# The opening of an attention kernel: batch 0 projected in plain fp32, with one token tile's queries ahead of it

## The chip, the cores and the metric

The program runs on one core of a Trainium2 chip. The metric is the device time of one launch, in microseconds (us): the median of three runs before the change is 610.33 us (609.41 to 612.26). Names of engines: PE is the tensor engine's matmul side and PEld its weight load, DVE is the vector engine, ACT the scalar engine, POOL the GpSimd engine, SP the sync engine, which here only issues loads and stores. ACT issues some loads as well.

## The reference

The program is one transformer-like block on `x` of 64 x 32 x 256 (64 batches of 32 tokens) and a context of 64 x 257 x 192, in three stages, each on a layer norm of `x` and added to it:

```
q = layernorm(x) @ Wq + bq           # 16 heads of 16
k = ctx @ Wk + bk ; v = ctx @ Wv + bv
attn = softmax(clip(q k^T / 4)) ; x = x + (attn v) @ Wo + bo
x = x + causal_attention_with_tanh(layernorm(x))     # second stage
x = x + mixture_of_8_experts(layernorm(x), top 2)    # third stage
```

Only the start of the first stage is touched here.

## The kernel before

The first stage goes over 64 batches `i`, one after the other. For one batch PE computes the scores (`scores(i)`, 16 instructions), weighs the values of batch `i-2` (`weigh`), transposes the probabilities of batch `i-1` (`transp`), and projects keys and values of batch `i+1` (`kproj`, `vproj`). DVE clips the scores, takes the negative maxima and copies half of the transposed probabilities; ACT computes the exponentials and moves keys, values and the other half out of PSUM; POOL spreads the queries over the heads' rows (`spread`, tile QF), handles the 257th key (`tailpart`, tile tm) and prepares the context.

In the loop keys and values are not multiplied as plain fp32. Context `cx` and weights `wA` are each cut into a high part (hA, wH) and a rest (lA, wL) of a faster format (fp32r), and five products stand for one (`terms`): 10 instructions for the keys and 10 for the values of a batch. The high parts are copies; the rests need a subtraction after them. `split(j, n)` on POOL does so for context pair `j` (two batches) in four steps n = 0 to 3: two high parts, the rest of channels 0 to 127, the rest of the last 64. A plain fp32 product is two instructions per pair of operands.

Ahead of the loop the kernel before does this. SP and ACT issue the loads in a written order; each has a queue of its own, and all share the core's 16 DMA engines. PE runs six products of 512 columns on a tile of ones (`warm(6)`). When the first four token tiles of `x` (512 tokens, batches 0 to 15) are there, DVE and POOL normalise them (`stats`, `rstd`, `xnorm`), PE turns them (`qturn(0)`), ACT copies them to `xnT` (`qchunk(0)`), PE computes the "x" row block, which is the 257th value of all batches, and then projects the queries of the 512 tokens (`qproj(0)`). DVE moves them to `qT` (`qevac(0)`). Only then do the projections of batch 0 follow, in the split form, and the loop starts. `base_row` is a small product of the output weights, done in iteration 0. The 257th values go to DRAM and come back spread over partitions (`load_tails`, tile Vt); POOL's `tailpart(0)` needs them.

Every engine runs its instructions in written order, and semaphores join the engines: `s_q`, `s_qe` for queries made and moved, `s_t0`, `s_t0e` for turned tokens, `s_wl` for the weights' rest, `s_lo` for the context's, `s_xn` for normalised token tiles. PSUM banks 4 to 7 go round in the order of the list `uses`; `take` on PE waits until the use four places earlier has been moved out.

## Time and profile before

| quantity | value |
|---|---|
| median of the runs | 610.33 us |
| time of the profiled execution | 609.9 us |
| its span, first to last instruction | 608.1 us |
| PE busy | 588.9 us (97% of the span) |
| DVE / ACT / POOL busy | 457.2 / 337.2 / 321.3 us |
| mean granted clock of PE | 0.994 |

The span and the time differ by 1.8 us, which lies around the instructions. In the page's 40 slices PE stands at 9 in each of the first 27, and the granted clock at 9 as well. So busy shares do not tell what bounds the opening; the chain of waits and the instructions in order of time do.

### The profile page before, as it was taken

The numbers are of one execution on the slowest core, as the hardware profiler recorded it, in microseconds if no ns is written. First come the engines' busy times: TensorE is split into PE (matmuls) and PEld (weight loads), VectorE is DVE, ScalarE is ACT, GpSimd is POOL, SyncE is SP. The second block draws the span as 40 slices with busy tenths as digits, with TensorE's granted clock in tenths as the row PEclk, the third lists the DMA queues.
The fourth block names the chain that finished last, engine by engine and source line by source line (L and its number), as shares of the span: only waits on it lengthen the run. The fifth ranks groups of instructions, "written<-read, shape, count | busy, mean of one in ns | idle before, by whom it ended". The sixth has DMA issues, their size and how long they took to land.

```text
span 608.1 us, 21788 instructions
## 1 busy us (share of the span) xinstructions
PE 588.9 (97%) x8367; PEld 482.3 (79%) x8367; DVE 457.2 (75%) x1069; ACT 337.2 (55%) x751; POOL 321.3 (53%) x474
## 2 busy tenths in 40 slices
PE   9999999999999999999999999998899999998977
PEld 4888878888788887888887788884588888884865
DVE  4688877888678886777777676888788888883654
ACT  3677868878687786777776156454323333330211
POOL 3457858787578777678874311111433333314771
PEclk9999999999999999999999999998999999999899
DMA  8724653776354855875400797257333334434884
GB/s 226 182 74 110 172 180 99 246 183 212 110 193 127 246 157 175 199 230 153 150 16 3 307 416 285 67 178 253 128 131 130 131 130 133 131 124 131 232 251 118
DMA packets 66069, 102.11 MB, mean 168 GB/s; under 512 B 15504, under 2 KB 42192, under 8 KB 65072
## 3 DMA queue, kind: packets, MB, share of 16 engines
q1 hardware_dynamic: 60672, 86.42, 44.2%
q0 software_dynamic: 4432, 13.50, 8.1%
q8 instruction: 69, 1.13, 0.8%
q10 hardware_dynamic: 864, 0.79, 0.5%
q14 instruction: 32, 0.26, 0.1%
HBM read 69.42 MB, written 31.26 MB: 166 GB/s over the span
## 4 chain that ended last, share of the span: by engine, by line
PE 54%; POOL 23%; issue 14%; DVE 3%; DMA 2%; ACT 2%; POOLq 0%; DVEq 0%; ACTq 0%
PE bank L1936 12%; PE scores L1936 6%; PE bank L1044 5%; PE bank L1051 5%; PE bank L1076 4%; POOL hA L718 4%; POOL lA L714 4%; POOL cg L1768 4%; POOL hA L710 4%; PE scores L1092 3%; PE scores L1065 3%; POOL Mb L751 2%; POOL tm L742 2%; PE bank L1961 1%; PE scores L1921 1%
## 5 line engine op out<-in xcount | busy, mean ns | idle before, releaser
L850 DVE TENSOR_SCALAR Pm<-scores 128x514 f32<-128x514 f32 x128 | 88.0, 688 | 52.8 <-PE scores L1065 52.6
L966 ACT ACTIVATE Pm<-Pm,nm 128x257 f32<-128x257 f32 x256 | 115.8, 505 | 2.5 <-DVE nm L855 2.5
L855 DVE TENSOR_REDUCE nm<-Pm 128x2 f32<-128x514 f32 x128 | 87.4, 683 | 2.2
L1757 POOL DMA_INDIRECT Xg<-y_d,inv x39 | 37.0, 950 | 82.9 <-PE scores L1921 70.1
L961 ACT ACTIVATE PT<-bank 128x512 f32<-128x512 f32 x64 | 38.3, 598 | 74.0 <-PE bank L1076 74.0
L1044 PE MATMUL bank<-hA,wH 128*128 128x258 f32 x256 | 75.2, 304 | 0.3 <-POOL hA L718 0.3
L1076 PE MATMUL bank<-cst,Pm 128*128 128x128 f32 x512 | 70.0, 279 | 0.0
L1044 PE MATMUL bank<-hA,wL 128*128 128x258 f32 x256 | 69.3, 281 | 0.0
L1051 PE MATMUL bank<-wH,hA 128*128 128x256 f32 x256 | 69.0, 281 | 0.0
L1051 PE MATMUL bank<-wL,hA 128*128 128x256 f32 x256 | 68.9, 280 | 0.0
L1895 ACT ACTIVATE sg<-sg 128x512 f32<-128x512 f32 x39 | 24.7, 632 | 77.6 <-DVE sg L1782 77.6
L1936 PE MATMUL bank<-W,xh 128*128 x208 | 66.7, 402 | 0.5 <-DVE xl L1849 0.5
L1092 PEld LDWEIGHTS scores<-Vs,PT 128*32 128x32 f32 x4096 | 41.2, 110 | 25.2 <-issue 24.1
L751 POOL TENSOR_TENSOR Mb<-Os,rc 128x64 f32<-128x64 f32 x64 | 21.6, 338 | 73.6 <-DVE rc L875 73.2
L1076 PEld LDWEIGHTS bank<-cst,Pm 128*128 128x128 f32 x512 | 54.9, 141 | 2.9 <-issue 0.8
L944 ACT ACTIVATE kT<-bank,bcol 128x258 f32<-128x258 f32 x128 | 53.5, 469 | 2.6 <-PE bank L1044 2.3
L1044 PEld LDWEIGHTS bank<-hA,wH 128*128 128x128 f32 x256 | 48.4, 189 | 1.2 <-issue 1.1
L1044 PEld LDWEIGHTS bank<-hA,wL 128*128 128x128 f32 x256 | 48.5, 189 | 0.2 <-issue 0.2
L1051 PEld LDWEIGHTS bank<-wL,hA 128*128 128x128 f32 x256 | 48.2, 188 | 0.0
L1051 PEld LDWEIGHTS bank<-wH,hA 128*128 128x128 f32 x256 | 48.2, 188 | 0.0
L1092 PE MATMUL scores<-Vs,PT 128*32 128x17 f32 x4096 | 47.5, 186 | 0.2 <-issue 0.2
L1768 POOL DMA_INDIRECT cg<-g_d,pi x32 | 31.7, 992 | 26.5 <-DMA g_d<-gg 17.0
(280 smaller groups left out, 1434.1 us busy)
## 6 DMA issues: line engine op xcount, KB each, us to landing
w_d<-whl SPq DMA_DIRECT2D x64, 256.0 KB, 3.5
W<-w_d SPq DMA_DIRECT2D x6, 2048.0 KB, 16.7
g_d<-gg SPq DMA_DIRECT2D x39, 256.0 KB, 2.4
wst<-in_W1T SPq DMA_DIRECT2D x32, 256.0 KB, 3.3
cx<-in_ctxT SPq DMA_DIRECT2D x31, 258.0 KB, 3.0
cx<-in_ctxT SPq DMA_DIRECT2D x62, 129.0 KB, 3.5
bb<-in_b SPq DMA_DIRECT2D x8, 512.0 KB, 6.3
W<-w_d SPq DMA_DIRECT2D x5, 512.0 KB, 5.3
```

The lines of the kernel that those rows point to most:

```text
L850: v.tensor_scalar(Pm[:, i % 2, 2 * p:2 * p + 2, :], S4[:, 2 * p:2 * p + 2, 0:NK], -CLAMP, CLAMP, ALU.max, ALU.min).then_inc(s_cl, 1)
L855: v.tensor_reduce(nm[:, i % 2, 2 * p:2 * p + 2], Pm[:, i % 2, 2 * p:2 * p + 2, :], AX.X, ALU.max, negate=True).then_inc(s_nm, 1)
L944: a.activation(kT[:, i % 2, m, :], held("k", i, m)[:, 0:NKP], ACT.Identity, bias=bcol[:, 2 + m:3 + m]).then_inc(s_ke, 1)
L961: a.activation(PT[:, i % 2, 0, :, :].rearrange("p a b -> p (a b)"), held("p", i, 0)[:, :], ACT.Copy).then_inc(s_pte[0], 1)
L966: a.activation(Pm[:, i % 2, g, :], Pm[:, i % 2, g, :], ACT.Exp, bias=nm[:, i % 2, g:g + 1]).then_inc(s_ex, 1)
L1044: mm = t.matmul(b[:, 0:NKP], w[:, 128 * m:128 * m + 128], c, start=(e == 0), stop=(e == 4))
L1051: mm = t.matmul(b[:, C * c:C * c + C], x[:, 128 * c:128 * c + 128], w[:, C:2 * C], start=(e == 0), stop=(e == 4))
L1076: mm = t.transpose(b[:, o:o + 128], Pm[:, i % 2, 2 * p + gg, 128 * c:128 * c + 128], ident)
L1092: mm = t.matmul(pO[r, VH * g:VH * g + VH], PT[:, i % 2, p, 2 * gg + c, r], Vs[:, i % 4, c, 4 * (h // 2) + g, h % 2, :], start=first, stop= ...
L1757: g.indirect_dma_start(out=Xg[:, i % 3, :], out_offset=None, in_=y_d, in_offset=bass.IndirectOffsetOnAxis(ap=inv[:, i:i + 1], axis=0)).the ...
L1768: g.indirect_dma_start(out=cg[:, j % 8, k, :], out_offset=None, in_=g_d, in_offset=bass.IndirectOffsetOnAxis(ap=pi[:, k, j:j + 1], axis=0) ...
L1936: mm = t.matmul(o, x[:, i % 2, k, :], W1[:, bass.DynSlice(w + (part * 2048 + k * 1024 + 512 * h), 512)], start=(k == 0 and part == 0 and x ...
```

## The change

Batch 0 no longer goes through the split form. Its context (columns of batch 0 alone), the key and value weights in plain fp32 and the biases are loaded first, with one token tile of `x` (tokens 0 to 127, batches 0 to 3) right behind; PE projects keys and values of batch 0 from them (`first_projections`, two products of 128 and 64 rows each), then turns and projects that one token tile (`first_queries`), and scores(0) follow. `warm(6)` is `warm(2)`, and the `warm(1)` further on is gone. The "x" row block comes after scores(0), the other three token tiles are normalised, turned and projected between batches 0 to 2: their statistics in the middle of batch 0's DVE work, their turn at the end of PE's iteration 0 and their projection at the end of iteration 1. On POOL the high parts of context pair 0 are made as well (ACT did them), and the statistics of the three tiles go ahead of pair 1's rests. Some semaphores are merged and counts shifted, which moves nothing.

```diff
-                load_x(0)
-                sp.dma_start(cst[:, 0:C_MN], d["cst"][:, 0:C_MN]).then_inc(s_id, 16)
-                sp.dma_start(wA[:, 0, C:2 * C], d["Wv"][0:128, :]).then_inc(s_w, 16)
-                sp.dma_start(wA[0:64, 1, C:2 * C], d["Wv"][128:192, :]).then_inc(s_w, 16)
+                src = d["ctxT"]
+                sp.dma_start(cx[:, 0, 0, 0, :], src[0, 0:128, :]).then_inc(s_f, 16)
+                sp.dma_start(xa[:, 0, :], d["x"][0:4].rearrange("a b c -> (a b) c")).then_inc(s_fx, 16)
+                sp.dma_start(wA[0:64, 1, 0:C], d["Wk"][128:192, :]).then_inc(s_f, 16)
+                sp.dma_start(cst[:, 0:C_MN], d["cst"][:, 0:C_MN]).then_inc(s_c, 16)
+                sp.dma_start(bcol[:, :], d["bcol"]).then_inc(s_f, 16)
+                sp.dma_start(Wq[:, :, :], d["Wq"].rearrange("(k p) n -> p k n", p=128)).then_inc(s_c, 16)
+                sp.dma_start(wA[64:128, 1, 0:C], d["Wk"][128:192, :]).then_inc(s_w, 16)
+                sp.dma_start(wA[64:128, 1, C:2 * C], d["Wv"][128:192, :]).then_inc(s_w, 16)
                 sp.dma_start(c256[:, 0, :], d["c256"][0:128, :]).then_inc(s_w, 16)
                 sp.dma_start(c256[0:64, 1, :], d["c256"][128:192, :]).then_inc(s_w, 16)
-                sp.dma_start(Wq[:, :, :], d["Wq"].rearrange("(k p) n -> p k n", p=128)).then_inc(s_c, 16)
-                sp.dma_start(bcol[:, :], d["bcol"]).then_inc(s_c, 16)
-                sp.dma_start(wA[64:128, 1, C:2 * C], d["Wv"][128:192, :]).then_inc(s_w, 16)
+                sp.dma_start(xa[:, 1:4, :], d["x"][4:16].rearrange("(n a) b c -> (a b) n c", a=4)).then_inc(s_x[0], 16)
                 sp.wait_ge(s_cx[0], 48)
...
-                split(0, 2)
-                split(0, 3)
-                split(1, 2)
+                for n in range(3):
+                    split(0, n)
                 spread(0)
                 g.wait_ge(s_qb, 1)
+                split(0, 3)
+                spread(1)
+                g.wait_ge(s_qb, 2)
+                rstd(0)
+                split(1, 2)
                 split(1, 3)
                 for i in range(T + 2):
-                    if i + 1 < T:
+                    if 1 <= i < T - 1:
                         spread(i + 1)
...
                 v.memset(PT[:, 0, 0, :, :], 1.0).then_inc(s_fill, 1)
-                v.wait_ge(s_x[0], 16)
-                stats(0, 4)
-                v.wait_ge(s_mv, 4)
+                v.wait_ge(s_fx, 16)
+                stats(0, 1)
+                v.wait_ge(s_mv, 1)
                 v.wait_ge(s_rs, 1)
-                for n in range(4):
-                    xnorm(n)
-
+                xnorm(0)
+                first_qevac()
...
+                def first_tokens():
+
+                    v.wait_ge(s_vx, 1)
+                    v.wait_ge(s_v1, 1)
+                    for h in range(2):
+                        v.tensor_copy(vx[:, h, :, :, 0:16],
+                                      held("x")[0:T, 128 * h:128 * h + 128].rearrange("p (g s c) -> p s g c", g=4, s=2)
+                                      ).then_inc(s_vxe, 1)
+                    v.wait_ge(s_rs, 2)
+                    for n in range(1, 4):
+                        xnorm(n)
...
+                        if i == 0:
+                            v.wait_ge(s_x[0], 16)
+                            stats(1, 3)
...
                     if i == 0:
+                        first_tokens()
                         base_row()
+                    if i == 1:
+                        qevac(0)
...
+                def first_qchunk():
+                    a.wait_ge(s_t0, 1)
+                    a.activation(xnT[:, :, 0:128], held("first turn")[:, 0:256].rearrange("p (k n) -> p k n", k=2), ACT.Copy
...
-                src = d["ctxT"][0:2]
-                a.dma_start(cx[:, 0, 0, :, :], src[:, 0:128, :].rearrange("b p n -> p b n")).then_inc(s_cx[0], 16)
-                for h in range(2):
-                    a.dma_start(cx[64 * h:64 * h + 64, 0, 1, :, :], src[:, 128:192, :].rearrange("b p n -> p b n")
-                                ).then_inc(s_cx[0], 16)
...
-                highs(0)
-                qchunk(0)
-                a.wait_ge(s_w, 16 * 8)
-                a.activation(wH[:, :, :], wA[:, :, :], ACT.Copy).then_inc(s_wh, 1)
-                highs(1)
+                src = d["ctxT"]
+                a.dma_start(wA[:, 0, 0:C], d["Wk"][0:128, :]).then_inc(s_f, 16)
+                a.dma_start(cx[0:64, 0, 1, 0, :], src[0, 128:192, :]).then_inc(s_f, 16)
+                a.dma_start(wA[:, 0, C:2 * C], d["Wv"][0:128, :]).then_inc(s_fv, 16)
+                a.dma_start(wA[0:64, 1, C:2 * C], d["Wv"][128:192, :]).then_inc(s_fv, 16)
+                a.dma_start(cx[:, 0, 0, 1, :], src[1, 0:128, :]).then_inc(s_cx[0], 16)
+                a.dma_start(cx[0:64, 0, 1, 1, :], src[1, 128:192, :]).then_inc(s_cx[0], 16)
+                a.dma_start(cx[64:128, 0, 1, :, :], src[0:2, 128:192, :].rearrange("b p n -> p b n")).then_inc(s_cx[0], 16)
...
+                kevac(0, 0)
+                kevac(0, 1)
+                first_qchunk()
+                a.wait_ge(s_f, 80)
+                a.wait_ge(s_fv, 32)
+                a.wait_ge(s_w, 64)
+                a.activation(wH[:, :, :], wA[:, :, :], ACT.Copy).then_inc(s_wh, 1)
+                vevac(0)
+                highs(1)
...
-                warm(6)
+                warm(2)
...
+                def first_projections():
+
+                    t.wait_ge(s_f, 80)
+                    for m in range(2):
+                        b = take("k", 0, m)
+                        for k in range(2):
+                            K = 128 - 64 * k
+                            mm = t.matmul(b[:, 0:NKP], wA[0:K, k, 128 * m:128 * m + 128], cx[0:K, 0, k, 0, :],
+                                          start=(k == 0), stop=(k == 1))
+                        mm.then_inc(s_k, 1)
+                    t.wait_ge(s_fv, 32)
+                    b = take("v", 0)
+                    for c in range(2):
+                        for k in range(2):
+                            K = 128 - 64 * k
+                            mm = t.matmul(b[:, C * c:C * c + C], cx[0:K, 0, k, 0, 128 * c:128 * c + 128], wA[0:K, k, C:2 * C],
+                                          start=(k == 0), stop=(k == 1))
+                    mm.then_inc(s_v, 1)
+
+                def first_queries():
+
+                    t.wait_ge(s_c, 32)
+                    t.wait_ge(s_xn, 1)
+                    b = take("first turn")
+                    for k in range(2):
+                        mm = t.transpose(b[:, 128 * k:128 * k + 128], xa[:, 0, 128 * k:128 * k + 128], ident)
+                    mm.then_inc(s_t0, 1)
+                    t.wait_ge(s_t0e, 1)
+                    b = take("first q")
+                    for m in range(2):
+                        for k in range(2):
+                            mm = t.matmul(b[:, 128 * m:128 * m + 128], Wq[:, k, 128 * m:128 * m + 128], xnT[:, k, 0:128],
+                                          start=(k == 0), stop=(k == 1))
+                    mm.then_inc(s_q, 1)
+
...
+                def x_row():
+
+                    t.wait_ge(s_w, 64)
+                    b = take("x")
+                    for k in range(2):
+                        K = 128 - 64 * k
+                        mm = t.matmul(b[0:T, 0:C], c256[0:K, k, :], wA[0:K, k, C:2 * C], start=(k == 0), stop=(k == 1))
+                    mm.then_inc(s_vx, 1)
+
+                first_projections()
+                first_queries()
...
-                t.wait_ge(s_wl, 1)
-                for i in range(-1, T + 2):
-                    if 0 <= i < T:
+                for i in range(T + 2):
+                    if i < T:
                         scores(i)
+                    if i == 0:
+                        x_row()
+                        t.wait_ge(s_wl, 1)
...
+                    if i in turns:
+                        qturn(turns.index(i))
+                    if i - 1 in turns:
+                        qproj(turns.index(i - 1))
```

PE, from the warm-up to the first scores, or the first split product where these come later. `bank` is a PSUM bank, cst the unit matrix, c_79 the 257th context rows, hA and lA, wH and wL the parts. Before:

```order
L1003 MATMUL bank<-PT 128x512 x5
L1020 MATMUL bank<-cst,xb 128x128 [waits s_xn,s_id]
L1020 MATMUL bank<-cst,xb 128x128 [waits s_xn] x7
L1003 MATMUL bank<-PT 128x512
L1112 MATMUL bank<-wA,c_79 64x256 [waits s_w,s_c]
L1112 MATMUL bank<-wA,c_79 64x256
L1029 MATMUL bank<-xnT,Wq 128x512 [waits s_t0e]
L1029 MATMUL bank<-xnT,Wq 128x512
L1029 MATMUL bank<-xnT,Wq 128x512 [waits s_t0e]
L1029 MATMUL bank<-xnT,Wq 128x512
L1044 MATMUL bank<-hA,wH 128x258 [waits s_lo,s_t0e,s_wl]
```

Now:

```order
L1054 MATMUL bank<-PT 128x512
L1164 MATMUL bank<-cx,wA 128x258 [waits s_f]
L1164 MATMUL bank<-cx,wA 128x258 x3
L1172 MATMUL bank<-wA,cx 128x256 [waits s_fv]
L1172 MATMUL bank<-wA,cx 128x256 x3
L1182 MATMUL bank<-cst,xb 128x128 [waits s_xn,s_c]
L1182 MATMUL bank<-cst,xb 128x128
L1188 MATMUL bank<-xnT,Wq 128x128 [waits s_ke,s_t0e]
L1188 MATMUL bank<-xnT,Wq 128x128 x3
L1118 MATMUL scores<-kT,QF 64x258 [waits s_ke,s_qb]
L1118 MATMUL scores<-kT,QF 64x258 x7
L1198 MATMUL bank<-wA,c_79 64x256 [waits s_ke,s_w]
```

What stood before the first split product was the work of four token tiles and the "x" block; now plain projections and one token tile stand there, and the scores of batch 0 precede the "x" block. The turn of the three other tiles and their projection have gone behind `base_row` and behind the projections of batch 2.

DVE, around the work of batch 0. Pm and nm are its clipped scores and maxima, st and mv statistics, xb the tokens. Before:

```order
L816 TENSOR_SCALAR qT<-bank,bcol 128x512 [waits s_q] x2
L850 TENSOR_SCALAR Pm<-scores 128x514 [waits s_s]
L855 TENSOR_REDUCE nm<-Pm 128x2 [waits s_cl]
L850 TENSOR_SCALAR Pm<-scores 128x514 [waits s_s]
L855 TENSOR_REDUCE nm<-Pm 128x2 [waits s_cl]
L841 TENSOR_TENSOR base<-bank,bcc 128x256 [waits s_base,s_c2]
L850 TENSOR_SCALAR Pm<-scores 128x514 [waits s_s]
```

Now:

```order
L890 TENSOR_REDUCE nm<-Pm 128x2 [waits s_cl]
L885 TENSOR_SCALAR Pm<-scores 128x514 [waits s_s]
L825 BN_STATS st<-xb 128x6 [waits s_x0]
L825 BN_STATS st<-xb 128x6 x2
L828 BN_AGGR mv<-st 128x2 [waits s_st] x3
L890 TENSOR_REDUCE nm<-Pm 128x2 [waits s_cl]
L865 COPY vx<-bank 64x8x16 [waits s_v1,s_vx]
L865 COPY vx<-bank 64x8x16
L831 SCALAR_TENSOR_TENSOR xb<-xb,mv,rs 128x256 [waits s_rs]
L831 SCALAR_TENSOR_TENSOR xb<-xb,mv,rs 128x256 x2
L876 TENSOR_TENSOR base<-bank,bcc 128x256 [waits s_base,s_w3]
L885 TENSOR_SCALAR Pm<-scores 128x514 [waits s_s]
```

Statistics of three tiles stand between the clip and the second maximum of batch 0, and the "x" copies and three normalisations between that maximum and batch 1.

POOL, from the end of the first normalisation to the loop. Before:

```order
L714 TENSOR_TENSOR lA<-cx,hA 128x516 [waits s_hi,s_cx0,s_rs]
L718 TENSOR_TENSOR hA<-cx,hA 64x516 [waits s_lo]
L714 TENSOR_TENSOR lA<-cx,hA 128x516 [waits s_hi,s_cx1,s_lo]
L728 TENSOR_TENSOR QF<-qT,cst 128x128 [waits s_qe]
L718 TENSOR_TENSOR hA<-cx,hA 64x516 [waits s_lo,s_qb]
L728 TENSOR_TENSOR QF<-qT,cst 128x128 [waits s_lo]
L728 TENSOR_TENSOR QF<-qT,cst 128x128 [waits s_s]
```

Now:

```order
L724 TENSOR_SCALAR hA<-cx 128x516 [waits s_f,s_cx0]
L724 TENSOR_SCALAR hA<-cx 128x516
L731 TENSOR_TENSOR lA<-cx,hA 128x516 [waits s_fhi,s_cx0]
L747 TENSOR_TENSOR QF<-qT,cst 128x128 [waits s_qe]
L735 TENSOR_TENSOR hA<-cx,hA 64x516 [waits s_lo,s_qb]
L747 TENSOR_TENSOR QF<-qT,cst 128x128 [waits s_lo]
L689 TENSOR_TENSOR rs<-mv,epw 128x3 [waits s_mv,s_qb]
L691 TENSOR_TENSOR rs<-rs,epw 128x3 [waits s_ep]
L731 TENSOR_TENSOR lA<-cx,hA 128x516 [waits s_hi,s_cx1,s_rs]
L735 TENSOR_TENSOR hA<-cx,hA 64x516 [waits s_lo]
```

The three tiles' rstd (lines 689, 691) waits for DVE's statistics, and the rests of pair 1 are queued behind it.

## Rows read from the trace of the kernel before

**Rows 1.** The chain that ended last, 0 to 60 us: start, us, what.

```profile
9.70 0.77 PE bank L1020 x5
...
12.47 3.63 PE bank L1029 x8
16.11 1.20 PE bank L1044 x10
17.30 1.18 PE bank L1051 x10
18.48 0.62 PE scores L1065 x16
...
21.67 0.86 PE bank L1122 x4
22.53 0.62 PE scores L1065 x16
23.15 1.02 PE bank L1076 x8
...
26.56 0.62 PE scores L1065 x16
```

**Rows 2.** Waits of PE, 16 to 326 us: us in total, times, longest.

```profile
PE scores L1065 <- POOL QF L728: 0.6, 2, 0.3
```

**Rows 3.** Weight loads of the warm-up in order of time: start, us.

```profile
1.44 0.50 PEld L1003 LDWEIGHTS bank<-PT 128*128 128x128 f32 x2 [1.44 <-DVE PT L819]
...
5.87 0.34 PEld L1003 LDWEIGHTS bank<-PT 128*128 128x128 f32 x1 [0.52 <-issue]
6.55 0.19 PEld L1003 LDWEIGHTS bank<-PT 128*128 128x128 f32 x1 [0.34 <-issue]
```

**Rows 4.** Loads of the opening: KB, us from issue to landing.

```profile
cst<-in_cst SPq DMA_DIRECT2D x1, 84.0 KB, 3.8
...
wA<-in_Wk ACTq DMA_DIRECT2D x1, 64.0 KB, 5.4
bcol<-in_bcol SPq DMA_DIRECT2D x1, 4.0 KB, 5.8
...
cx<-in_ctxT SPq DMA_DIRECT2D x1, 258.0 KB, 3.0
```

**Rows 5.** DMA issues on SP and ACT in order of time: start, us.

```profile
5.31 0.59 SPq L579 DMA_DIRECT2D wA<-in_Wv  x1
...
18.17 3.79 SPq L604 DMA_DIRECT2D Vt<-vx_d  x8
...
4.50 0.62 ACTq L933 DMA_DIRECT2D wA<-in_Wk  x1
```

**Rows 6.** DVE in order of time: start, us, line, tiles, idle time before.

```profile
4.76 1.40 DVE L802 BATCH_NORM_STATS2 st<-xb 128x6 f32<-128x256 f32 x4 [3.37 <-DMA xb<-in_x]
...
7.97 1.67 DVE L808 SCALAR_TENSOR_TENSOR xb<-xb,mv,rs 128x256 f32<-128x256 f32 x4 [1.53 <-POOL rs L688]
12.13 1.50 DVE L828 TENSOR_TENSOR wL<-wA,wH 128x1024 fp32r<-128x1024 f32 x1 [2.48 <-ACT wH L937]
13.55 0.47 DVE L832 COPY vx<-bank 64x128 f32<-64x128 f32 x2
...
19.15 0.69 DVE L850 TENSOR_SCALAR Pm<-scores 128x514 f32<-128x514 f32 x1 [2.25 <-PE scores L1065]
```

**Rows 7.** POOL and ACT in order of time, the same columns.

```profile
6.81 1.04 POOL L688 TENSOR_TENSOR rs<-rs,epw 128x4 f32<-128x4 f32 x1
9.91 1.29 POOL L714 TENSOR_TENSOR lA<-cx,hA 128x516 fp32r<-128x516 f32 x1 [2.05 <-ACT hA L922]
...
16.97 0.40 POOL L728 TENSOR_TENSOR QF<-qT,cst 128x128 f32<-128x128 f32 x1 [0.92 <-DVE qT L816]
...
23.38 1.23 POOL L710 TENSOR_SCALAR hA<-cx 128x516 fp32r<-128x516 f32 x2
...
10.06 1.09 ACT L917 ACTIVATE xnT<-bank 128x512 f32<-128x512 f32 x2 [0.33 <-PE bank L1020]
```

More of the change, by code:

```diff
@@ L224, in build @@
         pO = S4[:, 3, 272:272 + 4 * VH]
-        uses = [(("t", 0, k), s_t0e, k + 1) for k in range(2)] + [(("x",), s_vxe, 2)] + [(("q", 0, m), s_qe, m + 1) for m in range(2)]
-        for i in range(-1, T + 1):
+        turns = (0, 11, 27, 43)
+        uses = [(("k", 0, p), s_ke, p + 1) for p in range(2)] + [(("v", 0), s_ve, 1)]
+        uses += [(("first turn",), s_t0e, 1), (("first q",), s_qe, 2), (("x",), s_vxe, 2)]
+        for i in range(T + 1):
             if 1 <= i:
@@ L235, in build @@
                 uses += [(("b",), s_basee, 1)]
-            if 0 <= i < 48 and i % 16 == 11:
-                uses += [(("t", i // 16 + 1, k), s_t0e, 2 * (i // 16 + 1) + k + 1) for k in range(2)]
-            if 0 <= i < 48 and i % 16 == 12:
-                uses += [(("q", i // 16 + 1, m), s_qe, 2 * (i // 16 + 1) + m + 1) for m in range(2)]
+            if i in turns:
+                uses += [(("t", turns.index(i), k), s_t0e, 2 * turns.index(i) + k + 2) for k in range(2)]
+            if i - 1 in turns:
+                uses += [(("q", turns.index(i - 1), m), s_qe, 2 * turns.index(i - 1) + m + 3) for m in range(2)]
         spot = {u[0]: n for n, u in enumerate(uses)}
@@ L967, in exps @@
                                  ).then_inc(s_ex, 1)
-                for i in range(-1, T + 1):
+                kevac(0, 0)
[7 more added lines that the diff above has]
+                highs(1)
+                for i in range(T + 1):
                     if 1 <= i:
@@ L982, in _ @@
                         vevac(i + 1)
-                    if 0 <= i < 48 and i % 16 == 11:
-                        qchunk(i // 16 + 1)
+                    if i in turns:
+                        qchunk(turns.index(i))
                     q = (i - 8) // 3
@@ L1102, in busy @@
                                  skip_group_check=True)
-                t.wait_ge(s_id, 16)
-                qturn(0)
-                warm(1)
-                t.wait_ge(s_c, 32)
-                t.wait_ge(s_w, 16 * 8)
-                b = take("x")
-                for k in range(2):
-                    K = 128 - 64 * k
-                    mm = t.matmul(b[0:T, 0:C], c256[0:K, k, :], wA[0:K, k, C:2 * C], start=(k == 0), stop=(k == 1))
-                mm.then_inc(s_vx, 1)
-                qproj(0)
+                def first_projections():
[15 more added lines that the diff above has]
+                    mm.then_inc(s_v, 1)
@@ L1149, in _ @@
                         base_row()
-                    if 0 <= i < 48 and i % 16 == 11:
-                        qturn(i // 16 + 1)
-                    if 0 <= i < 48 and i % 16 == 12:
-                        qproj(i // 16 + 1)
+                    if i in turns:
+                        qturn(turns.index(i))
+                    if i - 1 in turns:
+                        qproj(turns.index(i - 1))
             @block.sync
```

101 lines of the change are left out of this document (56 added, 45 removed).

## The prediction

> **What bounds the kernel now.** I read three views. The chain of waits tells which engine's work ended last at each moment. From 9.70 us on it lies on PE without a break: the turn of four token tiles, the query projection of 512 tokens at 12.47 (eight instructions, 3.63 us), keys and values of batch 0 from 16.11 to 18.48, then scores(0) at 18.48, scores(1) at 22.53 and scores(2) at 26.56 [rows 1]. The waits say the same of the loop: from 16 to 326 us PE's longest entry is 0.6 us over two waits [rows 2]. So the loop of 64 batches is pure PE time, and a change of the opening is worth what it moves scores(2) by, the first scores behind which both programs have the same work left. Everything is settled in the first 28 us, and I read DVE, POOL, ACT and the loads there in order of time.
>
> The measure is therefore the start of scores(2): 26.56 us before.
>
> **When the first product can start now.** It waits for five loads, the biases last of SP's. Issues follow one another by about 0.55 us (SP's ninth ends at 5.9, having begun at 0.72) [rows 5], so the biases are issued near 2.9. A load issued in the opening crowd takes 3.8 us (84 KB) to 5.8 us (the biases themselves, behind 1.1 MB on their queue), and 3.0 us (258 KB) when the crowd has passed [rows 4]. With 0.41 MB ahead of it on its queue I take the quickest, 3.0: the start is at 5.9, bounds 5.9 and 8.7. It can't be before 4.9, where the warm-up ends: two products are four instructions of 512 columns, one per 0.85 us from 1.44 on [rows 3]. The value weights, issued fourth on ACT near 3.2, land at 6.2 to 8.6, inside or just behind the key projection.
>
> **What the first projections cost.** Plain fp32 has eight instructions for the keys and eight for the values, 256 or 258 columns. Four of 256 columns took 0.86 us (line 1122) [rows 1], 0.215 each, so 3.44 us at the high clock; the split form took 1.20 + 1.18 = 2.38. The plain form is 1.06 us dearer on PE, and is bought for an earlier start. The clock matters more. The warm-up's weight loads stand 0.85 us apart up to 5.87 and take 0.34 us, and take 0.19 from 6.55 [rows 3]: by that pace PE runs at its lower level (1.2 GHz) for some 4.8 us of unbroken work from 1.44 and at 2.4 GHz afterwards, though the granted clock reads 0.99 for the whole. In the old opening that slow stretch was filler and cost nothing. Now PE works to 4.9, stands idle for a microsecond and then does real work. If the rise comes at 6.6 all the same, the sixteen instructions end at 5.9 + 3.44 + 0.35 = 9.7. If it takes another 4.8 us from 5.9, eleven run at 0.43, and they end at 11.7. No row shows which; I take a rise at 8.0 (about five instructions at 0.43, eleven at 0.215), ending at 10.4, nearer the early end because the filler still counts for something.
>
> The Trainium skill's page "TensorE: Matmul & The Clock Gate", section "What's actually happening", says that "the default state is throttled, and activity releases the throttle." The trace agrees in that the pace doubles only after sustained work, and it speaks against cutting the warm-up from six to two. By that rule alone the late end, 11.7, would hold.
>
> **One token tile's queries.** Two turns at 0.128 (eight took 1.02) [rows 1]: 10.65. ACT copies 256 columns, two of 512 took 1.09 [rows 7], so 0.35: 11.05. Eight instructions of 128 columns, 0.128 each as for the turns: 12.1. DVE moves two blocks of 128 columns, as the two copies at 13.55, 0.5 us [rows 6]: 12.7. POOL's spread takes 0.40 [rows 7]: scores(0) starts at 13.2, hand-overs included. Beside this, POOL first makes two high parts (1.23) and one rest (1.29) [rows 7], from a load whose last piece is issued near 5.1 on ACT (the sixth of before was at 4.50 [rows 5]) and takes up to 5.4 us [rows 4]: done by 13.0 at the latest, so at worst 0.3 us late. The tile's normalisation (loads at about 5, then 0.35 + 0.1 + 0.3 + up to 1.04 + 0.42) ends by 7.3 and is covered by the projections. So scores(0) comes 5.3 us earlier than at 18.48.
>
> **What is owed afterwards.** The work that stood ahead of it comes between. After scores(0) at 13.2: scores 0.62, the "x" block 0.86 (four instructions of 256 columns like line 1122), keys and values of batch 1 2.38, `base_row` 0.86: PE is at 17.9. The rest of the weights must be there for batch 1's keys at 14.7: DVE has it at 12.7 + 1.50 = 14.2 [rows 6], POOL the context's at 13.2 + 1.28 = 14.5. Both just fit. wL also needs ACT's wH, whose last load is SP's tenth, issued near 5.9 and at most 5.8 us on its way: 11.7, plus half the price of ACT's two copies of 512 columns per 512, 1.1 for 1024, is 12.8, so in the worst case the keys come 0.1 late.
>
> Then PE must turn three token tiles, six times 0.128, and here it waits. DVE's chain: wL to 14.2, clip, maximum, clip (0.69 each, overlapping by 0.1) to 16.2, statistics of three tiles 1.05 (four took 1.40) and 0.3: 17.5. POOL's rstd, 0.2 and up to 1.04 (no row has three columns; four took 1.04, and I take that): 18.9. DVE fills the time with batch 0's second maximum and the "x" copies, then normalises three tiles at 0.42 (four took 1.67): 20.15 [rows 6, 7]. The second round of turns can only follow the third tile, so PE is through at 20.7 instead of 18.7. This is a new wait of 2.0 us, and behind it in PE's order stand scores(1).
>
> From 20.7: scores(1) 0.62, transposes 1.02, keys and values of batch 2 2.38, the projection of 384 tokens 2.6 (three quarters of 3.63 is 2.7; eight instructions at 0.32 are 2.6). scores(2) start at 27.3. POOL's rests of pair 1, queued behind the rstd, end at 18.9 + 2.6 = 21.5, ahead of 22.3 where they are wanted.
>
> Sum: 27.3 - 26.56 = +0.75 us. Check by amounts: the real work starts 3.8 us earlier (9.70 to 5.9). Against it stand 1.06 for the plain form and 0.2 for the small query products, 1.06 for the lower clock, 1.5 for the hand-overs between the first tile's turn and scores(0), and 2.0 for the three tiles' wait; 1.3 of filler and load waits, which the old stretch from 9.70 to 26.56 held beside 15.6 of work, falls away. That gives +0.7. The profiled execution (609.9, span 608.1 and 1.8 around it) becomes 610.65; the median of the runs is 0.43 above it, so I forecast 611.1.
>
> The other new order is hidden. The "x" copies end near 18.6 rather than 14.0. In the old trace the eight tail loads were issued by 21.96 (18.17 + 3.79) [rows 5], 7.9 behind the copies; now 26.5, and batch 2's first clip, which needs tile tm, is due at 28.0. That leaves about 1.2 us.
>
> **Rivals.**
> A. The loads land late and the clock is late: slower. Place: the first product's wait. If the biases take the 5.8 us of their own row, the start is 8.7, PE has been idle for 3.8 us, and eleven instructions run at the lower level: projections end at 14.5, 4.1 later than I take, everything behind shifts, and scores(2) start at 31.4, which is 615.2. For it: every load issued after 2.9 in the old opening took over 5 us, as the biases' and the key weights' rows show. Against: the queues carry much less ahead of these. It decides from a projection end of 12.7, where the loss passes 3.05 us.
>
> The Trainium skill's page "DMA: Bandwidth & Descriptors", section "Bandwidth", has the rule: "Transfers under 64 KB are descriptor-dominated." The rows agree that the 4 KB load was no quicker than one of 64 KB (5.8 against 5.4). This adds to A's chance and not to its price.
>
> B. The three tiles' wait does not arise and the clock rises early: faster. The projections end at 9.7 (-0.7), the loads at 4.9 (-1.0), and POOL and DVE are through with the tiles when PE arrives (-2.0 in full). All three together give 26.56 - 2.95, or 607.4; the early clock and half the wait give 609.4. For it: the chain of DVE is long but each piece is an estimate. Against: DVE's chain hangs on the same first scores as PE's, so an earlier start moves both and closes nothing.
>
> C. The 257th values come late: their round through DRAM takes 3 us more than 7.9. Then batch 2's clip waits 1.8 us, and PE behind it, 612.9.
>
> D. Nothing shows: losses and gains cancel within 0.3 us, 610.3. This belongs to the forecast's own range.
>
> **How the numbers follow.** The forecast with D has 0.65, A 0.13, B 0.15, C 0.07. A change of this kernel can be told from none at about 0.5%, or 3.05 us: below 607.3 or above 613.4. The forecast, its early clock (610.4) and late clock (612.4), C and nearly all of B lie inside. Faster is what B reaches at its full length, 0.06. Slower is A, nearly whole, with a sliver of C beside a late clock, 0.14. That leaves 0.80 within. The range goes from 608.2 (B in most parts) to 614.2 (A with half its delay).
>
> **What would show it.** In the new profile: the first fp32 product at 5.9, the pace of its instructions (0.43 or 0.215), scores(0) at 13.2, a wait of PE at line 1073 for DVE's normalised tiles of about 2 us, scores(1) at 20.7 and scores(2) at 27.3, and the same distances from there on. It is wrong if PE waits at batches 2 to 4, if that wait is missing, or if scores(2) differ from 27.3 by more than 2 us.

## The result and the profile after

The changed kernel takes 620.06 us, median of four runs (616.77 to 621.05), against 609.87 before (608.21 to 612.26; the 610.33 given ahead of the prediction was the median of the first three): ratio 1.0145, 95% interval 1.0112 to 1.0178. It is slower, and 5.9 us above the upper end of the forecast's range. The profiled execution took 620.06 with a span of 618.2. scores(2) start at 37.10 instead of 26.56 [rows 1], 10.5 us later. That is the whole difference of 10.2, and from there on the batches follow at the same distances as before. So the measure was the right one, and the size of every step ahead of it decides.

The chain that ended last (start, us, what) in the new kernel:

```profile
4.85 4.54 DMA cx<-in_ctxT
...
12.12 6.92 issue
...
19.07 1.32 POOL QF L747
...
20.43 1.18 PE scores L1118 x16
...
26.20 2.57 DVE xb L831 x2
...
29.84 0.66 PE bank L1073 x4
30.49 0.62 PE scores L1118 x16
...
37.10 0.62 PE scores L1118 x16
```

Before, the chain lay on PE from 9.70 on [rows 1]. Now it passes through POOL's spread (QF) and DVE's normalisation (xb), the hand-over ahead of scores(0) and the one that the change moved between scores(0) and scores(1). In the stretch from 12.12 the view stays with POOL, which has nothing to do there; QF's own row below names DVE's qT as what it waits for, and qT waits for PE's queries, which end at 18.34. So PE's work of the opening is on the path up to there. PE in order of time (start, busy us, line, tiles, idle time before):

```profile
5.88 4.69 PE L1164 MATMUL bank<-cx,wA 128*128 128x258 f32 x8 [0.65 <-DMA bcol<-in_bcol]
10.51 4.67 PE L1172 MATMUL bank<-wA,cx 128*128 128x256 f32 x8
15.11 0.69 PE L1182 MATMUL bank<-cst,xb 128*128 128x128 f32 x2
16.27 2.07 PE L1188 MATMUL bank<-xnT,Wq 128*128 128x128 f32 x8 [0.47 <-ACT xnT L963]
20.43 1.17 PE L1118 MATMUL scores<-kT,QF 32*64 32x258 f32 x16 [2.09 <-POOL QF L747]
21.53 2.16 PE L1198 MATMUL bank<-wA,c 128*64 128x256 f32 x4
...
23.99 0.42 PE L1097 MATMUL bank<-hA,wL 128*128 128x258 f32 x1
...
27.32 0.28 PE L1104 MATMUL bank<-wH,lA 128*128 128x256 f32 x1
...
27.68 1.02 PE L1209 MATMUL bank<-Wo,bcol 128*128 128x256 f32 x4
...
29.30 0.33 PE L1073 MATMUL bank<-cst,xb 128*128 128x128 f32 x1 [0.49 <-DVE xb L831]
29.84 0.66 PE L1073 MATMUL bank<-cst,xb 128*128 128x128 f32 x4 [0.21 <-DVE xb L831]
```

The sixteen plain instructions last from 5.88 to 15.11, 9.2 us. Scores(0) take 1.18 where they took 0.62 [rows 1], split products 0.42 each up to 27.1 and 0.28 behind it: PE runs at its lower level (1.2 GHz) for the first 21 us of its real work, while the granted clock of the profile reads 1.00 throughout. The first change of the clock that this trace records is the rise at 27.2, and ahead of it the view shows 1.00. A second profile of the same kernel, e11 below, records a change early on, and its granted clock is 0.50 where the same instructions take the same times. Stretch, its length, busy us of PE, PEld, DVE, ACT and POOL, granted clock, share and GB/s of DMA, in the kernel after, then in e11:

```profile
5.88:15.11 9.23, 9.23 (x17) 4.00 (x17) 0.00 (x0) 0.95 (x2) 2.49 (x3) 1.00 0.85 233
```

```profile
7.70:16.00 8.30, 7.83 (x16) 3.52 (x17) 0.00 (x0) 1.86 (x4) 2.50 (x3) 0.50 0.79 228
```

The weight loads of the first pairs show a second loss:

```profile
5.88 0.50 PEld L1164 LDWEIGHTS bank<-cx,wA 128*128 128x128 f32 x2 [2.23 <-DMA bcol<-in_bcol]
7.04 0.50 PEld L1164 LDWEIGHTS bank<-cx,wA 64*128 64x128 f32 x2 [0.66 <-issue]
8.19 0.50 PEld L1164 LDWEIGHTS bank<-cx,wA 128*128 128x128 f32 x2 [0.66 <-issue]
```

A plain product is a pair of instructions. One pair takes 1.155 us, and two instructions of 256 columns at the lower level take 0.86. The missing 0.30 is a weight load that isn't hidden: from pair to pair the operands change between 128 and 64 rows. DVE and POOL, the same columns:

```profile
18.91 1.22 DVE L858 TENSOR_TENSOR wL<-wA,wH 128x1024 fp32r<-128x1024 f32 x1
...
26.20 3.58 DVE L831 SCALAR_TENSOR_TENSOR xb<-xb,mv,rs 128x256 f32<-128x256 f32 x3 [0.38 <-POOL rs L691]
```

```profile
19.07 1.31 POOL L747 TENSOR_TENSOR QF<-qT,cst 128x128 f32<-128x128 f32 x1 [6.95 <-DVE qT L847]
...
25.27 0.89 POOL L691 TENSOR_TENSOR rs<-rs,epw 128x3 f32<-128x3 f32 x1
26.24 1.30 POOL L731 TENSOR_TENSOR lA<-cx,hA 128x516 fp32r<-128x516 f32 x1
27.61 1.34 POOL L735 TENSOR_TENSOR hA<-cx,hA 64x516 fp32r<-64x516 f32 x1
```

The spread took 0.40 before [rows 7]; now it begins 0.16 us behind wL and ends 0.25 behind wL's end. Four normalisations took 1.67 [rows 6]; three take 3.58, beside the rests of pair 1.

### The profile page after: what moved, and what is told of

Read it like the earlier page. It is cut to its first block, busy times and chain, and to the rows that moved or that the text cites. A ratio compares the mean times of both kernels' runs of the same rounds, so it can differ in the third digit from the quotient of the medians.

```text
span 618.2 us, 21790 instructions
## 1 busy us (share of the span) xinstructions
PE 595.5 (96%) x8361; PEld 483.3 (78%) x8361; DVE 459.2 (74%) x1071; ACT 336.4 (54%) x750; POOL 324.3 (52%) x478
## 4 chain that ended last, share of the span: by engine, by line
PE 48%; POOL 24%; issue 16%; DVE 8%; DMA 2%; ACT 2%; POOLq 0%; ACTq 0%; DVEq 0%
PE bank L2025 12%; PE scores L2025 6%; PE bank L1097 4%; PE bank L1104 4%; POOL cg L1857 4%; PE bank L1129 4%; POOL lA L731 4%; POOL hA L735 4%; POOL hA L724 4%; PE scores L1118 3%; PE scores L1145 3%; POOL Mb L770 2%; POOL tm L761 2%; PE scores L2010 1%; POOL whl L804 1%
## 5 line engine op out<-in xcount | busy, mean ns | idle before, releaser
L1118 PE MATMUL scores<-kT,QF 32*64 32x258 f32 x1024 | 44.7, 406 | 2.7 <-POOL QF L747 2.7
```

The lines of the kernel that those rows point to most:

```text
L1118: mm = t.matmul(B[g][64 * m:64 * m + 64, 0:NKP], QF[r, i % 2, m, :], kT[r, i % 2, m, :], start=True, stop=True, skip_group_check=True)
```

## The experiments

They ran on chips where the kernel before takes 629.2 to 629.4 us (the profiles of e3 and e7, which are that kernel with one change each, have the extra time in the last stage: behind line 1936 they have 76 us left, and the kernel before has 59 on the first chip; the distances between scores(0), (1) and (2) are as before), so each ratio is to the kernel before on the same chip. Starts of scores(0), (1), (2) are from each profile; "by start" is 629.3 plus what scores(2) start after 26.56, an estimate of the time from one profile. In the last two rows scores(2) lack a projection of 2.6 us that comes a batch later; it is added.

| run | median us | ratio (95%) | scores(0), (1), (2) | by start |
|---|---|---|---|---|
| e11_after_here | 636.36 | 1.0107 (1.0076–1.0138) | 19.7, 29.7, 36.3 | 639.1 |
| e1_warm6 | 636.84 | 1.0119 (1.0077–1.0160) | 18.2, 27.8, 34.4 | 637.1 |
| e2_warm4 | 634.57 | 1.0097 (1.0065–1.0129) | 15.6, 25.6, 32.3 | 635.0 |
| e3_before_warm2 | 631.38 | 1.0043 (1.0021–1.0066) | 20.2, 24.2, 28.2 | 631.0 |
| e4_grouped | 637.67 | 1.0120 (1.0066–1.0175) | 20.0, 30.1, 36.7 | 639.5 |
| e9_rows128 | 632.51 | 1.0065 (1.0044–1.0086) | 14.3, 23.9, 30.5 | 633.3 |
| e5_filled | 634.59 | 1.0086 (1.0062–1.0110) | 15.6, 25.9, 32.5 | 635.2 |
| e6_ports | 632.74 | 1.0063 (1.0040–1.0086) | 15.4, 24.2, 31.7 | 634.4 |
| e7_plain_only | 633.32 | 1.0069 (1.0047–1.0091) | 21.0, 25.0, 29.1 | 631.8 |
| e10_split_back | 638.85 | 1.0167 (1.0146–1.0187) | 20.3, 30.2, 36.8 | 639.5 |
| e8_all_mended | 631.51 | 1.0030 (1.0009–1.0051) | 14.9, 22.6, 27.3 + 2.6 | 632.7 |
| e12_reordered | 631.88 | 1.0041 (1.0020–1.0063) | 14.5, 19.3, 26.0 + 2.6 | 631.4 |

The last column agrees with the medians within 1.8 us for all but the unaltered kernel (2.7). That one's four runs were 634.0, 634.2, 638.5 and 639.3, and the profile is of the longest, which the estimate meets to 0.2; e4's four spread from 634.1 to 639.8 in the same way, and its profile is of the longest too. No profile of a quick execution of either was taken.

**The warm-up.** e1_warm6 and e2_warm4 alter one number, e3_before_warm2 makes the cut alone, in the kernel before:

```diff
-                warm(2)
+                warm(6)    (e1; warm(4) in e2)
-                warm(6)
+                warm(2)    (e3, kernel before)
```

> The changed kernel with the warm-up of before (six products instead of two). Theory (clock): the whole loss, 10.5 us at the start of scores(2), comes from PE staying at its lower level (1.2 GHz) from 5.9 to 27.1 us because the short warm-up never raised it. With six products the pace rises near 6.2 as in the kernel before, the plain products start near 8.7 and run at half the time (16 at 0.29 = 4.6 us, to 13.3), scores(2) start near 30 and the run takes about 613.5. Rival (products): the plain products with their gaps don't hold the level wherever they stand; the pace falls back to the lower level after the warm-up, scores(2) start near 37 and the run takes 620 or more.

> The changed kernel with four warm-up products. Theory (clock): the pace rises near 6.2, inside the seventh or eighth of eight instructions; the warm-up ends at 7.3, the plain products end near 11.9, scores(2) start near 28.8: about 612. Rival (products): as for six, 620. A second rival (size of the gap): what counts is whether PE ever stands idle before the rise; then this one behaves as with six, 1.5 us earlier.

> The kernel before with two warm-up products instead of six. Theory (clock): the first real work at 9.1 then runs at the lower level; turns, x block and the 512-column query products cost twice as much until the pace rises. If it rises 4.8 us into the 512-column products the loss is 2 to 4 us (612 to 614); if it stays low as in the changed kernel, 8 us (618). Rival (no clock): the warm-up is filler, and the time stays at 610.

Weight loads of e2:

```profile
4.78 0.19 PEld L1054 LDWEIGHTS bank<-PT 128*128 128x128 f32 x1 [0.27 <-issue]
...
6.06 0.19 PEld L1164 LDWEIGHTS bank<-cx,wA 128*128 128x128 f32 x1 [0.24 <-DMA bcol<-in_bcol]
...
7.02 0.29 PEld L1164 LDWEIGHTS bank<-cx,wA 64*128 64x128 f32 x2 [0.34 <-issue]
7.65 0.30 PEld L1164 LDWEIGHTS bank<-cx,wA 128*128 128x128 f32 x2 [0.34 <-issue]
```

All sixteen run at 2.4 GHz, from 6.49 to 11.42, 4.9 us instead of 9.2, and scores(0) come 4.1 us before e11's. In all six profiles with a warm-up of four or more and the plain form (e1, e2, e5, e6, e8, e12) they do so; of the four with two, only e9's. When the level rises differs from execution to execution: the first weight load of 0.19 us stands at 4.8 in e2, e5 and e7, at 5.7 in e12, at 6.4 in e6, at 6.5 in e1 and the kernel before, at 6.6 in e8 and at 7.5 in e10. Two products end at 5.2, ahead of most of these. So the cut of the warm-up is what leaves the projections' level to the execution. Behind them the level falls in both, in e2 during the 2.1 us wait for the spread, in e1 near 19.9, as the split products begin; scores(2) start at 32.3 and 34.4, not at the 28.8 and 30 expected, because the rest of the loss remains. With six products in e1 the filler also holds the first plain product back to 9.1; against e2 that costs 2.6 us at scores(0).

The medians do not show a gain: e11, unaltered, has 636.36, between e2's 634.57 and e1's 636.84, and the intervals overlap. Two of e11's four executions took 634, as e2's five did; that these two ran the plain products at the higher level is likely and was not profiled.

In e3 the same cut costs the kernel before 1.7 us at scores(2) and 2.2 at the median, clear of the noise (2 to 4 us were expected): there too the low stretch reaches real work (its pace rises near 13.4).

**The rows of the operands.** e4_grouped orders the same products by rows, so the row count changes three times instead of seven; e9_rows128 has 128 rows everywhere; it leaves the last 64 context channels out of batch 0 and counts the first 128 twice.

```diff
+                    bk = [take("k", 0, m) for m in range(2)]
+                    for k in range(2):
+                        for m in range(2):
...
-                        for k in range(2):
+                        for e, k in enumerate((1 - c, c)):
```

> The changed kernel with the plain products in another order: the products of 128 rows and those of 64 rows are grouped, so that the number of rows changes 3 times instead of 7. Theory (weight load): each change of the row count leaves a weight load of 0.3 us uncovered, which is why a pair of instructions takes 1.155 us instead of 0.853; with the grouping the sixteen take about 9.23 - 4 x 0.30 = 8.0 us, and everything behind comes 1.2 us earlier: 618.8. Rival (256 columns): at the lower level every pair of 256 columns pays 0.3, whatever the rows; the sixteen take 9.2 and the time stays at 620. If the denser stream raises the clock, 614 or less.

```diff
-                            mm = t.matmul(b[:, 0:NKP], wA[0:K, k, 128 * m:128 * m + 128], cx[0:K, 0, k, 0, :],
+                            mm = t.matmul(b[:, 0:NKP], wA[:, 0, 128 * m:128 * m + 128], cx[:, 0, 0, 0, :],
```

> The changed kernel (two warm-up products) in which the second half of each plain product reads the operands of the first half, 128 rows instead of 64; the last 64 context channels are thereby left out of batch 0's keys and values and the first 128 counted twice. Theory (row count): with no change of the row count no weight load stays uncovered: a pair of 256-column instructions takes 0.853 us at the lower pace, the sixteen 6.9 us instead of 9.2. Rival: the pair still takes 1.155. For the pace itself: if it rises within this stream of full products, about 5 us after it begins, the sixteen end near 12 and scores(2) start near 33; if it stays low as with the 64-row products, near 34.7.

e4's sixteen take 6.67 to 14.71, 8.04 us instead of 9.23: four changes fewer, 1.19 us, 0.30 each, as expected. Scores(0) still start no earlier than in e11, whose first four instructions ran at the higher level and whose sixteen take 8.03 as well, and the median is no better. At the higher level (e12) the same order takes 4.15 instead of 4.93, 0.20 each. e9's PE:

```profile
6.41 2.01 PE L1163 MATMUL bank<-cx,wA 128*128 128x258 f32 x8 [1.21 <-DMA bcol<-in_bcol]
8.25 1.89 PE L1170 MATMUL bank<-wA,cx 128*128 128x256 f32 x8
```

They end by the next turn at 9.98, 3.6 us from 6.41 on: an instruction takes 0.22, near the 0.215 of the prediction, for products of one row count at the higher level. e9 was also at that level from its first product, with warm(2). That isn't an effect of the rows alone, for the unaltered kernel, e11_after_here, began at it too:

> The changed kernel itself, unaltered, on the same chip as the other experiments, so that their ratios can be set beside its own. Every theory expects 1.014 to 1.017 of the kernel before and scores(2) near 37.

```profile
6.31 0.30 PEld L1164 LDWEIGHTS bank<-cx,wA 128*128 128x128 f32 x2 [2.65 <-DMA bcol<-in_bcol]
...
7.57 0.36 PEld L1164 LDWEIGHTS bank<-cx,wA 128*128 128x128 f32 x2 [0.34 <-issue]
8.59 0.50 PEld L1164 LDWEIGHTS bank<-cx,wA 64*128 64x128 f32 x2 [0.66 <-issue]
```

In that execution two pairs ran at 0.63, the third took 1.02 and the rest 1.155: the level fell inside the third, and the granted clock falls to 0.50 at 7.7, with PE working without a stop, where e2 and e9 kept theirs. In the kernel after, in e4 and in e11 it is then low to 27 or 28; in e9 it is low from 15.7 to 22.

**The plain form alone.** e7_plain_only gives the kernel before the plain products for batch 0, and nothing else of the change (one later load is moved to keep their operands).

```diff
+                    if i == 0:
+                        for k in range(2):
+                            K = 128 - 64 * k
+                            mm = t.matmul(b[:, 0:NKP], wA[0:K, k, 128 * m:128 * m + 128], cx[0:K, 0, k, 0, :],
```

> The kernel before, its warm-up, loads and four-tile queries as they were, with only batch 0's keys and values in plain fp32 (load_ctx(2) is issued after these products, since they read the plain context). Theory (weight load): at the high pace sixteen instructions with a change of the row count between pairs take 16 x 0.29 = 4.6 us to 5.0 against 2.38, so scores(2) start 2.3 to 2.6 us later: 1.0040. Rival (columns alone): 16 x 0.215 = 3.44, 1.1 us later.

```profile
12.45 3.70 PE L1030 MATMUL bank<-xnT,Wq 128*128 128x512 f32 x8
15.99 2.49 PE L1047 MATMUL bank<-cx,wA 128*128 128x258 f32 x8
18.41 2.58 PE L1061 MATMUL bank<-wA,cx 128*128 128x256 f32 x8
20.92 0.69 PE L1081 MATMUL scores<-kT,QF 32*64 32x258 f32 x16
```

At the higher level the sixteen take 4.93 us where the split form took 2.38 [rows 1], +2.5, and scores(0) to (2) are late by that. The prediction had +1.06. The median is 3.9 above the kernel before. PE stands still for another 1.3 us ahead of 31.9, with no engine named as what it waits for; whether that is the rest of the median is not shown, for the profiled execution itself is 2.6 above (632.04).

**Who decides scores(1).** e5_filled adds to e2 products that nobody reads (two behind the first queries, four ahead of the turn), so that the pace never falls.

```diff
+                        if c == 0 and k == 0:
+                            fill(b[:, :], 4)
...
+                    fill(B[0][:, :], 2)
```

> The kernel with four warm-up products (e2_warm4), and PE kept at work in its two long waits: two 512-column filler products behind the first queries' projection, four ahead of the turn of the three tiles (they write a bank that is overwritten afterwards). Theory (chain): the pace stays high from 6 us on, but behind the first queries the start of scores(1) hangs on DVE and POOL (scores(0), clip, wL, statistics, rstd, three normalisations), so only the first scores' shorter duration is won: scores(1) start 0.4 to 0.8 us earlier than e2's 25.6, scores(2) near 31.6, 4.6 to 5.2 us above the kernel before. Rival (clock): the lower pace between 15.6 and 22 us is most of e2's remaining loss of 5.7 us; then scores(2) start below 29 and the loss is under 2.5 us.

```profile
20.91 3.56 DVE L831 SCALAR_TENSOR_TENSOR xb<-xb,mv,rs 128x256 f32<-128x256 f32 x3 [0.38 <-POOL rs L691]
```

```profile
21.62 3.60 PE L1161 MATMUL bank<-PT 128*128 128x512 f32 x8
25.05 0.82 PE L1075 MATMUL bank<-cst,xb 128*128 128x128 f32 x6
```

From scores(0) to scores(1) it takes 10.2 us, in e2 with its pace falling 10.0. The filler itself costs some of that: the third normalisation ends at 24.47, and the turn starts behind the filler at 25.05. From the start of scores(0) to the end of the normalisations it is 8.8 us here and 9.3 in e2. So PE's pace is worth 0.5 us in this stretch, the difference between scores(0) of 0.71 and of 1.18, and the rest is DVE's and POOL's chain, which ends with three normalisations of 3.56.

e6_ports is e2 with DVE's wL held until the first spread is done, and POOL's rests of pair 1 until the normalisations are:

```diff
+                g.wait_ge(s_xn, 4)
...
+                v.wait_ge(s_qb, 1)
```

> e2_warm4 with DVE and POOL kept from working at the same time at two places: DVE's wL waits until POOL has spread batch 0's queries, and POOL's rests of pair 1 wait until DVE has normalised the three tiles. Theory (contention): the spread takes 0.40 instead of 1.31 us and the three normalisations 1.25 instead of 3.58; scores(0) start 0.9 earlier, scores(1) 3.0 earlier (22.6), PE then waits about 0.5 for the rests of pair 1, and scores(2) start near 29.7: 3 us above the kernel before. Rival (these operations are slow for another reason, the shape or PSUM): both keep their durations, the waits only add, and the loss is 6 to 7 us.

```profile
15.44 2.34 DVE L860 TENSOR_TENSOR wL<-wA,wH 128x1024 fp32r<-128x1024 f32 x1 [0.58 <-POOL QF L747]
...
22.24 1.28 DVE L832 SCALAR_TENSOR_TENSOR xb<-xb,mv,rs 128x256 f32<-128x256 f32 x3 [0.38 <-POOL rs L691]
```

```profile
14.93 0.40 POOL L747 TENSOR_TENSOR QF<-qT,cst 128x128 f32<-128x128 f32 x1 [1.69 <-DVE qT L848]
15.41 1.28 POOL L735 TENSOR_TENSOR hA<-cx,hA 64x516 fp32r<-64x516 f32 x1
```

The spread is back at 0.40 and the three normalisations at 1.28, so both had been waiting for the other engine. The same shows where it was moved to: wL, begun 0.03 us behind a rest of 1.28, takes 2.34 instead of 1.22. The Trainium skill's page "SBUF — State Buffer", section "SBUF: two separate sides", says that GpSimd and a DVE instruction with two inputs from SBUF share ports under an exclusive lock, and that the loser blocks until the other is through. The trace agrees: wL ends 1.1 us behind the end of the rest that was ahead of it, and in the kernel after QF ends 0.25 behind wL's end, neither more than the second one's own duration (1.22 and 0.40). Of the 3.2 us freed, 0.6 reach scores(2) against e2: the filler of this execution ran longer at the lower level, so the first product starts 0.7 later (7.21), and PE now waits 0.6 for wL, 1.6 for the "x" copies and 0.6 for a late rest. The expectation had scores(2) at 29.7; they start at 31.7.

**The queries' part alone.** e10_split_back keeps the single token tile and returns batch 0 to the split form, with warm(6).

```diff
-                  first_projections()
+                  t.wait_ge(s_wl, 1)
+                  for p in range(2):
+                      kproj(0, p)
+                  vproj(0)
```

> The changed kernel with its loads, one token tile first and the rest between batches, but batch 0 in the split form as before and six warm-up products: the plain part undone alone. Theory (the queries' part loses by itself): keys and values wait for wL and the context's rest near 15, scores(0) start near 17.4, the chain over DVE and POOL to the three tiles' turn takes its 9.5 us to scores(1) as with six warm-ups, scores(2) near 34: 7 us above the kernel before. Rival (the plain form is the culprit): scores(2) near 28, 1 to 2 us above the kernel before.

```profile
13.37 2.13 POOL L736 TENSOR_TENSOR hA<-cx,hA 64x516 fp32r<-64x516 f32 x1
```

```profile
PE bank L1097 <- POOL hA L736: 4.0, 1, 4.0
```

scores(0) start at 20.3, later than before and than the 17.4 expected: PE waits 4.0 us for the context's last rest on POOL, which itself takes 2.13 instead of 1.28 beside wL, and behind that wait the split products run at the lower level, 4.55 us instead of 2.38. Without the plain form the operands, made in series on POOL, are too late for an early start.

**Mended versions.** Both have warm(4) and grouped products, hold wL behind the first spread (e12 behind both), let POOL make the rests of pair 1 ahead of the three tiles' rstd, and turn the three tiles a batch later; e8 has one filler product behind the first queries; e12_reordered, without it, puts the "x" block into the wait for the spread, makes all parts of pair 0 ahead of it, and moves `base_row` and the statistics.

```diff
-        turns = (0, 11, 27, 43)
+        turns = (1, 11, 27, 43)
...
+                v.wait_ge(s_qb, 1)     (s_qb, 2 in e12)
```

> The changed kernel with every loss found so far taken out: four warm-up products, the plain products grouped by rows, wL behind the spread, one filler product in the wait for it, and the three tiles' rstd after the rests of pair 1 with their turn in iteration 1 and their projection in iteration 2 (so nothing on PE waits for them). Theory: scores(0) near 13.7, scores(2) near 23.7 with 2.6 us of query projection still owed behind them, that is 26.3 against 26.5 of the kernel before: the same time within 0.5 us. If another wait takes their place, 2 to 4 us slower.

> The changed kernel with what the experiments showed put right: four warm-up products; plain products grouped by rows; the x block in the wait for batch 0's spread queries; POOL makes all of pair 0's parts before that spread; wL waits for both spreads; base_row after batch 2's projections, so it needs no bank that DVE still holds; statistics of the three tiles at the end of DVE's batch 0, their normalisation in batch 1, turn at the end of PE's iteration 1, projection in iteration 2. Theory (sum of the parts measured): plain products from 6.5 to 10.5, scores(0) near 14, scores(2) near 24.3 with 2.6 us owed behind it, so 26.9 less what the x block saves: 0.5 to 2 us faster than the kernel before, ratio 0.997 to 0.999. Rival (some other wait of this opening takes its place, as with e8): 1.002 or more.

The waits of PE up to 40 us (us in total, times, longest) in e8, then in e12:

```profile
PE bank L1217 <- DVE vx L866: 1.5, 1, 1.5
PE bank L1055 <- DVE PT L850: 1.4, 1, 1.4
PE bank L1098 <- DVE wL L859: 0.6, 1, 0.6
```

```profile
PE bank L1104 <- DVE wL L860: 1.1, 1, 1.1
PE bank L1218 <- DVE PT L902: 0.9, 1, 0.9
```

They give back two thirds of the loss, and neither beats the kernel before (1.003 and 1.004, both intervals above 1); e12's theory, 0.997 to 0.999, missed. Read from the rows, and not parted by further runs, what stays is 1.8 us of dearer plain products (4.15 in e12 against 2.38), the uncovered pass from the first tile over ACT, PE, DVE and POOL to scores(0), and waits for DVE, which has the opening's work of before in a shorter stretch.

## Why the prediction was wrong

Profiled forecast and profile of after, in us from step to step:

| step | forecast | measured | off by |
|---|---|---|---|
| first plain product | 5.9 | 5.88 | 0.0 |
| plain products | 4.5 | 9.2 | +4.7 |
| their end to scores(0) | 2.8 | 5.3 | +2.5 |
| scores(0) to scores(1) | 7.5 | 10.1 | +2.6 |
| scores(1) to scores(2) | 6.6 | 6.6 | 0.0 |

- **"When the first product can start now" was right**, to 0.02 us. It took the quickest load of the old rows, and in this profile the biases landed after 3.0. Rival A's place, late loads, did not occur. Three profiles of the same head on the other chips start at 6.3, 6.4 and 6.7, so that meeting the bound to 0.02 was partly luck.
- **"What the first projections cost" failed, twice.** *The clock:* the step took a rise at 8.0, with 11.7 as its late bound, because PE had taken 4.8 us of unbroken work to rise [rows 3]. That was one execution's value; the others' rises lie between 4.8 and 7.5 on the clock of the trace. In the kernel after it rose at 27.1. Neither bound held the outcome, since both let the level rise within the step and stay. e11's fall at 7.7 under load shows that this is no safe assumption. The Trainium skill's page "TensorE: Matmul & The Clock Gate", section "What's actually happening", has activity release the throttle. By that rule the prediction put the end at 11.7; in this trace PE was busy for 9.2 us from 5.88 to 15.11 without a stop and stayed low, so the measurement decides against it. *The weight loads:* 0.215 an instruction came from line 1122, whose four instructions all have 128 rows. A row of the same chain, passed over, has two pairs of 128 and 64 rows:

```profile
11.33 1.15 PE bank L1112 x4
```

  0.575 a pair at the higher level instead of 0.43; by it the sixteen take 4.6, and e7 measured 4.93. At the lower level the eight gaps are 2.35. The lower level cost 3.44 where 1.06 was forecast, +2.4; with 2.35 that is the 4.7.
- **"One token tile's queries" was 2.5 short.** At the lower level the stretch is 1.2 longer than at the higher one (5.3 against e2's 4.2, with the same spread of 1.31), the spread took 0.9 more than forecast, and the hand-overs 0.4 more. The step set wL behind qT and the spread beside it, and added both at the durations that they have alone. e6 shows the cost.
- **"What is owed afterwards": the wait exists, its cause was half right.** PE came to the turn at 28.5, 8.1 behind scores(0) instead of 4.7, by the lower level, so the wait for DVE was 0.7 rather than 2.0. The normalisations' 3.58, forecast as 1.26, would have held it in any case: at high pace (e5) the normalisations still end 8.8 us behind the start of scores(0). POOL's three-column rstd took 0.89, inside the bound of 1.04.
- **"The other new order is hidden" was right:** PE waits for nothing in batches 2 to 4.
- **The rivals.** A had the lower level right and its duration (eleven instructions) wrong: it gave 615.2. B, C and D did not occur.

Had the clock been high throughout, as in e5, scores(2) would still start at 32.5, or near 31.9 without the 0.6 that e5's filler holds the turn back, 4.6 above the forecast: 0.6 from two more warm-up products, 1.5 from the row changes, 0.9 and 2.3 from the two collisions of DVE and POOL, less the forecast's 1.06 for a late clock, and small hand-overs. The sum was made of durations that were true where they were read and not where they were put.

## What to carry to other kernels

Filler work at the start of a kernel can be what raises PE's level ahead of the real work; before it is cut, price the real work at the lower level for its whole length, and not up to one assumed rise. Take a matmul's duration from rows with the same alternation of shapes, not from the same column count. When work is moved, list what runs on DVE and POOL in its new place: two-input fp32 instructions of both added up instead of overlapping, up to 3.3 times their own duration.

## What the runs showed of the hardware

- PE stayed at its lower level for 21 us (5.9 to 27.1) while busy for 18.7 of the 21.2, and the profile's granted clock read 1.00 up to the first change that the trace records (27.2); in e11, which records one at 7.7, it read 0.50. Ahead of the first recorded change the pace is to be read from weight loads (0.50 a pair against 0.30) and matmuls (0.42 against 0.28). The level also fell under unbroken work (e11, 7.7 us). In a warm-up that goes on long enough the first quick weight load stands between 4.8 and 7.5 us, by the execution. What decides between staying and falling stays open: e9, e11 and e2 are one profile each.
- A change between 128 and 64 rows of operands leaves part of a weight load uncovered: 0.30 us per change at 1.2 GHz (after, e4), 0.20 at 2.4 GHz (e2, e7, e12), none where the rows stay (e9, and line 1122's four of 0.215).
- DVE's instructions with two fp32 inputs from SBUF and POOL's instructions lengthened each other: POOL's spread from 0.40 to 1.31 (after), DVE's wL from 1.22 to 2.34 (e6), POOL's rest from 1.28 to 2.13 (e10), DVE's three normalisations from 1.28 to 3.58 (e6 against after). Holding one engine back until the other was through restored the durations (e6).
